# Second layer's channel products, mixing and outputs: one 64-wide tile per image in place of 128-wide blocks that hold two

## The chip, the cores and the metric

The kernel runs on one core of a Trainium2 chip. The metric is the device time of one execution in microseconds; three executions took 310.94, 724.87 and 310.22 us, median 310.94. A separate, profiled execution took 310.58 us; its span from the first to the last instruction is 308.0 us. All data are fp32.

## The reference

Sixteen images of 64 channels and 16 x 16 pixels (N = 256) go through four layers, each `x = x + layer(groupnorm(x))`. The change is in the second layer:

```python
keys    = softmax(Wk x + bk, over N);  queries = softmax(Wq x + bq, over C);  values = Wv x + bv
context = einsum('bkn,bvn->bkv', keys, values)           # 64 x 64 per image
eff     = conv1x1(Wr, br, einsum('bkv,bkn->bvn', context, queries))
# chan_att(L) = softmax( einsum('bcn,bdn->bcd', softmax(L, over N), L), over d ): 64 x 64 per image
att     = chan_att(x) + chan_att(x - G1) + chan_att(G1 - G2)   # G1, G2: blurred x
freq    = einsum('bcd,bcn->bdn', att, queries)
out     = w_dw[0] * eff + w_dw[1] * freq
```

Layer 3 ("het") is a 3 x 3 convolution on some channel groups, layer 4 an attention with 8 heads over quarters of the image.

## The kernel before

Two images share the 128 partitions (channels of image 0 on partitions 0 to 63, of image 1 on 64 to 127); `t` counts the 8 pairs of images, `j = t // 2` counts twos of them, and `g` is the group: `t` 0 to 3 is group 0, 4 to 7 is group 1. In this document and the prediction "an image t" means such a pair of images. Each engine gets its instructions in one fixed order, and a list `SCHEDULE` gives the order of the steps to all of them: group 1 follows group 0 three steps behind. Engines wait for each other by semaphores only. For the second layer the end of the list is: scores1 (t 0, 1), levels1 (j 3), scores1 (t 2, 3), levels_T (j 2), mix1 (j 0), levels_T (j 3), mix1 (j 1), scores1 (t 4, 5), out1 (t 0, 1), scores1 (t 6, 7), out1 (t 2, 3), mix1 (j 2), norm of group 0 for layer 3, mix1 (j 3), out1 (t 4 to 7), norm of group 1, het.

The steps that the change touches:

- `products(t)`, TensorE (L555 to L568): per t the three score matrices and the context, contracted over the 256 pixels in two halves of 128 (k). Each multiplication has 128 weight columns and 128 moving columns, so it also computes the 64 x 64 blocks *between* the two images, which nobody wants. All four results lie in one PSUM bank (4 x 128 columns). A fp32 multiplication shows up as two instructions in the profile.
- `scores_in(t)`, VectorE (L1016 to L1029): adds "apart" (-1e30 between the images, 0 inside an image) to the three score matrices and writes them to SBUF as `att`; multiplies the context by "own" (0 between the images) into `ctxT`; takes the row maxima of `att` and makes the bias of the exponential.
- `channel_softmax(t)`, ScalarE (L1328 to L1333): three exponentials in place in `att`, with row sums.
- `context_out(t)`, TensorE (L570 to L574): `ctxT` times Wr, a 128 x 128 block-diagonal matrix.
- `mixing(j)`, VectorE (L1031 to L1057): for two t in turn, the weighted sum of the three attentions, times w_dw[1], plus the context's product; result `mix2`, 128 x 128 and zero between the images. Ten operations of 128 columns.
- `out_product(t)`, TensorE (L585 to L589): `mix2` times the queries, 256 moving columns.
- `add_out1(t)`, VectorE (L1059 to L1062): adds it to X and takes the statistics (L790) for the next norm.

PSUM banks are handed out in turn by `claim(pe, key, reader's semaphore, value)`: six "bulk" banks and two "small" ones. TensorE, whose queue is in order, waits in `claim` until the bank's last reader has signalled. For products that reader is `ctxT_ready`, VectorE's copy of the context.

After a group's norm (L806 to L824, with a power on GpSimd, L1464, and the result in `xn_pad`), sixteen transfers from SyncE (L1547) and sixteen from ScalarE (L1410) copy shifted rows of `xn_pad` into `region`, group 0 first, half of each engine's sixteen per group; het (L620, L625) of a group waits for its rows. Other lines that appear in the rows: L986 and L987 level maxima, L1307 the level exponentials, L1292 copies of transposed levels, L443 the product y3 of the first layer (128*64 tiles), L709 the products with the values in layer 4 (128*64 tiles), L643 the projections of layer 4, L1393 its exponential.

Of the kernel before, what the change touches and what calls it, by code (L numbers as in the profile page):

```python
# [18 lines left out]
P = 128  # L19
C = 64  # L20
# [3 lines left out]
HW = W * W  # L24
# [3 lines left out]
NK = HW // P  # L28
# [4 lines left out]
NT = NP * AREA  # L33
MASKED = -1e30
ROWS = (W + 2) * W
# [6 lines left out]

CONST = [("pairavg", 128), ("pairavg_by_out", 128), ("to_by_out", 128), ("ident", 128), ("own", 128), ("apart", 128), ("fold", 64), ("lap1", 2 * HW),
         ("lap2", 2 * HW), ("headmask", 4), ("spread", NG * 128), ("spsel", 3 * 128), ("eye4", 32)]
# [76 lines left out]
def program(nc, x_in, const_in, weight_in, param_in, out):  # L121
# [11 lines left out]
    with ExitStack() as ctx:  # L133
# [85 lines left out]
        def tokens_of_pairs():  # L219
# [28 lines left out]
        e_lT = [tokens_of_pairs() for _ in range(3)]  # L248
        att = pairs(384, "p (t s c) -> p t s c", s=3)
        ctxT = pairs(128)  # L250

# [35 lines left out]
                 " qsub_ready qexp_ready   qsm_ready q_mm q_ready "  # L287
                 "lT_mm lT_ready l_mm  a_mm amask_ready ctxT_ready "
                 "amax_ready arec_ready att_ready cw_mm mix_ready y1out_mm  "
# [8 lines left out]
         qsub_ready, qexp_ready, qsm_ready, q_mm, q_ready,  # L298
         lT_mm, lT_ready, l_mm, a_mm, amask_ready, ctxT_ready,
         amax_ready, arec_ready, att_ready, cw_mm, mix_ready, y1out_mm,  # L300
# [44 lines left out]
        def _(pe):  # L345
# [209 lines left out]
            def products(t):  # L555

                j = t // 2
                pe.wait_ge(elT_ready[j // 2], level_step(j % 2, 2) + 1)
                pe.wait_ge(ekT_ready, j + 1)
                pe.wait_ge(vT_ready, j + 1)  # L560
                n = claim(pe, ("a", t), ctxT_ready, t + 1)
                for s in range(3):
                    for k in range(NK):
                        mm(bank(n, s * 128, (s + 1) * 128), e_lT[s][:, k, t, :], lT[s][:, k, t, :],  # L564
                           start=(k == 0), stop=(k == NK - 1))
                for k in range(NK):
                    last = mm(bank(n, 384, 512), vT[:, t, k, :], ekT[:, k, t, :], start=(k == 0), stop=(k == NK - 1))
                last.then_inc(a_mm, 1)  # L568

            def context_out(t):  # L570
                pe.wait_ge(ctxT_ready, t + 1)
                pe.wait_ge(row_ready, 1)
                n = claim(pe, ("cw", t), mix_ready, t + 1, "small")
                mm(bank(n, 0, 128), ctxT[:, t, :], wr_s, start=True, stop=True).then_inc(cw_mm, 1)  # L574

# [9 lines left out]
            def out_product(t):  # L585
                pe.wait_ge(mix_ready, t + 1)
                pe.wait_ge(q_ready, t // 2 + 1)
                n = claim(pe, ("y1out", t), x_ready[1], t + 1)
                mm(bank(n, 0, HW), mix2[:, t, 0:128], q1[:, t, :], start=True, stop=True).then_inc(y1out_mm, 1)  # L589

# [180 lines left out]
        def _(dve):  # L771
# [244 lines left out]
            def scores_in(t):  # L1016

                dve.wait_ge(a_mm, t + 1)
                n = where[("a", t)]
                v.tensor_tensor(att[:, t, :, :], bank(n, 0, 384).rearrange("p (s c) -> p s c", s=3),  # L1020
                                cst("apart").unsqueeze(1).broadcast_to([P, 3, 128]), ALU.add).then_inc(amask_ready, 1)
                v.tensor_tensor(ctxT[:, t, :], bank(n, 384, 512), cst("own"), ALU.mult).then_inc(ctxT_ready, 1)
                dve.wait_ge(amask_ready, t + 1)
                v.tensor_reduce(amax[:, t, :], att[:, t, :, :], X_AXIS, ALU.max).then_inc(amax_ready, 1)

                step(v.reciprocal(lrec[:, t, :], lsum[:, t, :]))
                dve.wait_ge(amax_ready, t + 1)
                v.scalar_tensor_tensor(out=abias[:, t, :], in0=amax[:, t, :], scalar=-1.0, in1=lrec[:, t, :],  # L1028
                                       op0=ALU.mult, op1=ALU.mult).then_inc(arec_ready, 1)  # L1029

            def mixing(j):  # L1031

                c = slice(2 * j, 2 * j + 2)
                ts = (2 * j, 2 * j + 1)
                dve.wait_ge(att_ready, 2 * j + 2)
                recs = mark(v.reciprocal(arec[:, c, :], asum[:, c, :]))
                krecs = mark(v.reciprocal(krec[:, c], ksum[:, c]))
                dve.wait_ge(dve_small, recs)
                at = {}
                for t in ts:  # L1040
                    at[t] = mark(v.tensor_scalar(mix[:, t, 0:128], att[:, t, 0, :], arec[:, t, 0:1], None, ALU.mult))
                for s in (1, 2):
                    for t in ts:
                        dve.wait_ge(dve_small, at[t])
                        at[t] = mark(v.scalar_tensor_tensor(out=mix[:, t, 0:128], in0=att[:, t, s, :],
                                                            scalar=arec[:, t, s:s + 1], in1=mix[:, t, 0:128],
                                                            op0=ALU.mult, op1=ALU.add))
                for t in ts:
                    dve.wait_ge(dve_small, at[t])
                    at[t] = mark(v.tensor_tensor(mix[:, t, 0:128], mix[:, t, 0:128], wt("w1_row"), ALU.mult))  # L1050
                dve.wait_ge(dve_small, krecs)
                for t in ts:
                    dve.wait_ge(cw_mm, t + 1)
                    dve.wait_ge(dve_small, at[t])
                    v.scalar_tensor_tensor(out=mix2[:, t, 0:128], in0=bank(where[("cw", t)], 0, 128),
                                           scalar=krec[:, t:t + 1], in1=mix[:, t, 0:128],
                                           op0=ALU.mult, op1=ALU.add).then_inc(mix_ready, 1)  # L1057
# [161 lines left out]
        def _(act):  # L1219
# [108 lines left out]
            def channel_softmax(t):  # L1328
                act.wait_ge(arec_ready, t + 1)
                for s in range(3):  # L1330
                    last = a.activation(att[:, t, s, :], att[:, t, s, :], ACT.Exp, scale=lrec[:, t, s:s + 1],  # L1331
                                        bias=abias[:, t, s:s + 1], accum_out=asum[:, t, s:s + 1])
                last.then_inc(att_ready, 1)  # L1333
# [260 lines left out]
def constants():  # L1594

    i = np.arange(P)
    same_group = (i[:, None] // 2 == i[None] // 2) * 0.5
    own = (i[:, None] // C == i[None] // C) * 1.0
    y, x = np.divmod(np.arange(HW), W)
# [25 lines left out]
    for b in range(2):  # L1625
        for dx in range(3):
            spsel[3 * b + dx, dx, b * C:(b + 1) * C] = 1.0
    const = pack(CONST, {
        "ident": np.eye(P), "pairavg": same_group, "own": own, "apart": (1.0 - own) * MASKED,
        "fold": np.concatenate([np.eye(64)] * 2), "lap1": chunks(np.eye(HW) - b1), "lap2": chunks(b1 - b2),  # L1630
        "headmask": (i[:, None] % 32 // HD == np.arange(4)[None]) * 1.0,
# [97 lines left out]
```

## Time and profile before

| | |
|---|---|
| median of the runs | 310.94 us |
| profiled execution | 310.58 us |
| its span | 308.0 us |
| TensorE busy (matmul) | 232.2 us, 75% |
| VectorE busy | 194.8 us, 63% |
| ScalarE busy | 131.0 us, 43% |
| GpSimd busy | 35.9 us, 12% |
| chain that ended last | PE 50%; DVE 26%; issue 7%; ACT 5%; DMA 5%; POOL 4% |
| mean granted TensorE clock | 0.887 of full |

By stages, in microseconds from the span's start: the first layer and the start of the second run to about 117, the rest of the second layer to 160.2, layer 3 with its transfers to 187, and layer 4 to 308. PE, DVE, ACT, POOL, SP are the profile's names for TensorE, VectorE, ScalarE, GpSimd and SyncE. Busy times of successive instructions of one engine overlap by up to 0.1 us, so the distance from start to start is the better price of an instruction.

### The profile page before, as it was taken

The numbers are of one execution on the slowest core, as the hardware profiler recorded it, in microseconds if no ns is written. First come the engines' busy times: TensorE is split into PE (matmuls) and PEld (weight loads), VectorE is DVE, ScalarE is ACT, GpSimd is POOL, SyncE is SP. The second block draws the span as 40 slices with busy tenths as digits, with TensorE's granted clock in tenths as the row PEclk, the third lists the DMA queues.
The fourth block names the chain that finished last, engine by engine and source line by source line (L and its number), as shares of the span: only waits on it lengthen the run. The fifth ranks groups of instructions, "written<-read, shape, count | busy, mean of one in ns | idle before, by whom it ended". The sixth has DMA issues, their size and how long they took to land.

```text
span 308.0 us, 5530 instructions
## 1 busy us (share of the span) xinstructions
PE 232.2 (75%) x2032; PEld 141.4 (46%) x2032; DVE 194.8 (63%) x533; ACT 131.0 (43%) x322; POOL 35.9 (12%) x64
## 2 busy tenths in 40 slices
PE   0476997464599869989745378739998998997963
PEld 0355654133274754979622122223564463563541
DVE  3672343537279794797977125576497698686772
ACT  1026579100065577794700022236665565641510
POOL 1750000000100100000011502129001011000000
PEclk9999799755599999997965599997999999997995
DMA  6900000000000000000009990454025025000000
GB/s 223 405 4 3 0 3 0 0 0 2 0 0 0 3 0 0 3 0 2 1 10 228 216 213 5 106 128 108 3 52 124 0 50 135 27 17 20 2 34 34
DMA packets 9642, 16.67 MB, mean 54 GB/s; under 512 B 1936, under 2 KB 8208, under 8 KB 9360
## 3 DMA queue, kind: packets, MB, share of 16 engines
q1 hardware_dynamic: 8848, 13.75, 16.3%
q10 hardware_dynamic: 768, 2.58, 4.0%
q8 instruction: 16, 0.26, 0.4%
q14 instruction: 10, 0.08, 0.1%
HBM read 4.87 MB, written 1.05 MB: 19 GB/s over the span
## 4 chain that ended last, share of the span: by engine, by line
PE 50%; DVE 26%; issue 7%; ACT 5%; DMA 5%; POOL 4%; ACTq 2%; SPq 0%; DVEq 0%; POOLq 0%
PE psum L663 7%; PE psum L518 5%; PE psum L691 4%; DMA region<-xn_pad 4%; PE psum L709 4%; PE psum L681 3%; DVE xn_pad L1136 3%; PE psum L643 3%; DVE smax L1142 3%; POOL small L1464 2%; PE psum L479 2%; PE psum L564 2%; PE psum L414 2%; PE psum L506 2%; PE psum L625 2%
## 5 line engine op out<-in xcount | busy, mean ns | idle before, releaser
L1399 ACT ACTIVATE region<-psum 128x512 f32<-128x512 f32 x32 | 19.0, 594 | 30.8 <-PE psum L691 30.7
L1142 DVE TENSOR_REDUCE smax<-psum 128x8 f32<-128x512 f32 x32 | 21.9, 685 | 12.3 <-PE psum L681 12.3
L1464 POOL TENSOR_TENSOR small<-small 128x4 f32<-128x4 f32 x8 | 8.1, 1018 | 175.4 <-DVE small L808 175.4
L663 PE MATMUL psum<-region,w 128*32 128x512 f32 x160 | 23.0, 647 | 4.1 <-DVE region L1117 4.1
L1393 ACT ACTIVATE region<-region 128x512 f32<-128x512 f32 x32 | 20.1, 627 | 12.8 <-DVE region L1149 12.8
L790 DVE BATCH_NORM_STATS2 small<-X 128x6 f32<-128x256 f32 x32 | 12.5, 422 | 17.5 <-ACT X L1269 16.5
L691 PEld LDWEIGHTS psum<-const,region 128*128 128x128 f32 x128 | 14.3, 145 | 17.8 <-issue 11.8
L1149 DVE TENSOR_TENSOR region<-psum,smax 128x512 f32<-128x512 f32 x32 | 22.1, 690 | 0.6
L691 PE MATMUL psum<-const,region 128*128 128x128 f32 x128 | 21.2, 289 | 1.1 <-ACT region L1399 1.0
L709 PE MATMUL psum<-region 128*64 128x18 f32 x512 | 20.5, 214 | 0.0
L709 PEld LDWEIGHTS psum<-region 128*64 128x64 f32 x512 | 17.4, 137 | 5.2 <-issue 5.2
L1269 ACT ACTIVATE X<-psum,small 128x256 f32<-128x256 f32 x8 | 3.4, 470 | 37.5 <-PE psum L625 37.5
L625 PE MATMUL psum<-region,weight 128*32 128x512 f32 x96 | 12.6, 663 | 6.8 <-DMA region<-xn_pad 6.8
L643 PE MATMUL psum<-region,weight 128*128 128x512 f32 x24 | 13.2, 646 | 3.3 <-DVE small L816 3.3
L354 PE MATMUL psum<-small,const 128*128 128x8 f32 x16 | 3.6, 297 | 15.2 <-DVE small L797 9.9
L1331 ACT ACTIVATE region<-region,small 128x128 f32<-128x128 f32 x24 | 11.6, 488 | 6.8 <-DVE small L1028 6.8
L518 PE MATMUL psum<-region,const 128*128 128x512 f32 x32 | 14.2, 598 | 0.0
L1136 DVE SCALAR_TENSOR_TENSOR xn_pad<-v_pad,small,xn_pad 128x256 f32<-128x256 f32 x32 | 14.1, 487 | 0.0
L564 PE MATMUL psum<-region 128*128 128x128 f32 x96 | 13.3, 293 | 0.0
L564 PEld LDWEIGHTS psum<-region 128*128 128x128 f32 x96 | 12.6, 210 | 0.1
L1279 ACT ACTIVATE region<-psum 8x256 f32<-8x256 f32 x2 | 0.7, 373 | 27.9 <-PE psum L479 27.9
L354 PEld LDWEIGHTS psum<-small,const 128*128 128x128 f32 x16 | 3.3, 251 | 18.5 <-DVE small L797 12.6
(169 smaller groups left out, 490.9 us busy)
## 6 DMA issues: line engine op xcount, KB each, us to landing
region<-v_pad SPq DMA_DIRECT2D x64, 80.0 KB, 2.1
region<-xn_pad SPq DMA_DIRECT2D x16, 157.5 KB, 6.8
region<-xn_pad ACTq DMA_DIRECT2D x16, 157.5 KB, 6.6
weight<-weight_in SPq DMA_DIRECT2D x1, 1376.0 KB, 12.6
const<-const_in SPq DMA_DIRECT2D x1, 1330.0 KB, 9.9
X<-x SPq DMA_DIRECT2D x4, 256.0 KB, 5.2
out<-xn_pad SPq DMA_DIRECT2D x8, 128.0 KB, 1.7
weight<-weight_in SPq DMA_DIRECT2D x1, 918.0 KB, 6.7
```

Of the source, the lines that this page charges most:

```text
L518: last = mm(bank(n), lap[s][:, k, jn * 128:(jn + 1) * 128], xT[:, k, 4 * g:4 * g + 4, :].rearrange("p t c -> p (t c)"), start=(k == 0), st ...
L564: mm(bank(n, s * 128, (s + 1) * 128), e_lT[s][:, k, t, :], lT[s][:, k, t, :], start=(k == 0), stop=(k == NK - 1))
L625: last = mm(bank(n)[32 * q:32 * q + 32, :], hetW[:, q % 2, dx, :], rows[:, q, 2 * jj:2 * jj + 2, 0:W, dx:dx + W], start=False, stop=(dx == 2),
L643: mm(bank(n), wt(w), xn3[:, 2 * j:2 * j + 2, :].rearrange("p t n -> p (t n)"), start=True, stop=True)\
L663: last = mm(bank(n)[32 * c:32 * c + 32, :], w4[:, c % 2, dx, :], v4[:, j % 2, c, :, :, dx:dx + W], start=(dx == 0), stop=(dx == 4), tile_p ...
L691: last = tr(bank(n, q * 128, (q + 1) * 128), e3[:, w % NE, q * 128:(q + 1) * 128], ident)
L709: last = mm(dst[half, a2, b, h:h + 2, :].rearrange("p h e -> p (h e)"), e3T[:, w % NE, at + 64 * c:at + 64 * c + 64], va[:, 4 * t + 2 * a2 ...
L1136: v.scalar_tensor_tensor(out=a, in0=win, scalar=pe_w[:, 5 * PE_ROWS + i:5 * PE_ROWS + i + 1], in1=prev, op0=ALU.mult, op1=ALU.add).then_in ...
L1142: v.tensor_reduce(smax[:, w, :], src, X_AXIS, ALU.max).then_inc(smax_ready, 1)
L1149: v.tensor_tensor(s_sub[:, w % NE, :].rearrange("p (h m) -> p h m", h=HEADS), src, smax[:, w, :].unsqueeze(2).broadcast_to([P, HEADS, AP_] ...
L1393: a.activation(e3[:, u % NE, :], s_sub[:, u % NE, :], ACT.Exp, scale=HD ** -0.5).then_inc(e3_ready, 1)
L1399: a.activation(e3T[:, u % NE, :], bank(where[("e3T", u)]), ACT.Copy).then_inc(e3T_ready, 1)
```

## The change

`products` now issues each multiplication twice, once per image: 64 weight columns and 64 moving columns of that image, K = 128, into the partitions of that image, with the tile position (0, 64 b). The four results take 4 x 64 columns of the bank. `context_out` and `out_product` issue two 64 x 64 multiplications on the diagonal of the array, tile position (64 b, 64 b), both into the same bank. The blocks between images exist no more, so the mask, the multiplication by "own" and the semaphore `amask_ready` go; VectorE takes the maxima straight from PSUM (192 columns) and copies the context (64 columns); ScalarE reads the scores from PSUM. `att`, `ctxT`, `mix`, `mix2` are 64 columns wide per matrix, and so is every operation of `mixing`. The bank of the products is now released by `att_ready` (ScalarE's exponentials). The constants "own", "apart" and "fold" (320 columns, 0.16 MB) are no longer loaded.

```diff
@@ def products(t):
-                n = claim(pe, ("a", t), ctxT_ready, t + 1)
-                for s in range(3):
+                n = claim(pe, ("a", t), att_ready, t + 1)
+                operands = [(e_lT[s][:, :, t, :], lT[s][:, :, t, :]) for s in range(3)] + [(vT[:, t, :, :], ekT[:, :, t, :])]
+                for s, (left, right) in enumerate(operands):
                     for k in range(NK):
-                        mm(bank(n, s * 128, (s + 1) * 128), e_lT[s][:, k, t, :], lT[s][:, k, t, :],
-                           start=(k == 0), stop=(k == NK - 1))
-                for k in range(NK):
-                    last = mm(bank(n, 384, 512), vT[:, t, k, :], ekT[:, k, t, :], start=(k == 0), stop=(k == NK - 1))
+                        for b in range(2):
+                            half = slice(C * b, C * b + C)
+                            last = mm(bank(n, s * C, (s + 1) * C)[half, :], left[:, k, half], right[:, k, half],
+                                      start=(k == 0), stop=(k == NK - 1), tile_position=(0, C * b))
@@ def context_out(t):
-                mm(bank(n, 0, 128), ctxT[:, t, :], wr_s, start=True, stop=True).then_inc(cw_mm, 1)
+                for b in range(2):
+                    half = slice(C * b, C * b + C)
+                    last = mm(bank(n, 0, C)[half, :], ctxT[half, t, :], wr_s[half, half], start=True, stop=True,
+                              tile_position=(C * b, C * b))
+                last.then_inc(cw_mm, 1)
@@ def out_product(t):
-                mm(bank(n, 0, HW), mix2[:, t, 0:128], q1[:, t, :], start=True, stop=True).then_inc(y1out_mm, 1)
+                for b in range(2):
+                    half = slice(C * b, C * b + C)
+                    last = mm(bank(n, 0, HW)[half, :], mix2[half, t, 0:C], q1[half, t, :], start=True, stop=True,
+                              tile_position=(C * b, C * b))
+                last.then_inc(y1out_mm, 1)
@@ def scores_in(t):
-                v.tensor_tensor(att[:, t, :, :], bank(n, 0, 384).rearrange("p (s c) -> p s c", s=3),
-                                cst("apart").unsqueeze(1).broadcast_to([P, 3, 128]), ALU.add).then_inc(amask_ready, 1)
-                v.tensor_tensor(ctxT[:, t, :], bank(n, 384, 512), cst("own"), ALU.mult).then_inc(ctxT_ready, 1)
-                dve.wait_ge(amask_ready, t + 1)
-                v.tensor_reduce(amax[:, t, :], att[:, t, :, :], X_AXIS, ALU.max).then_inc(amax_ready, 1)
+                v.tensor_reduce(amax[:, t, :], bank(n, 0, 3 * C).rearrange("p (s c) -> p s c", s=3), X_AXIS, ALU.max)\
+                    .then_inc(amax_ready, 1)
+                v.tensor_copy(ctxT[:, t, :], bank(n, 3 * C, 4 * C)).then_inc(ctxT_ready, 1)
@@ def mixing(j): every 0:128 becomes 0:C, for example
-                    at[t] = mark(v.tensor_scalar(mix[:, t, 0:128], att[:, t, 0, :], arec[:, t, 0:1], None, ALU.mult))
+                    at[t] = mark(v.tensor_scalar(mix[:, t, 0:C], att[:, t, 0, :], arec[:, t, 0:1], None, ALU.mult))
@@ def channel_softmax(t):
-                    last = a.activation(att[:, t, s, :], att[:, t, s, :], ACT.Exp, scale=lrec[:, t, s:s + 1],
+                    last = a.activation(att[:, t, s, :], bank(where[("a", t)], s * C, (s + 1) * C), ACT.Exp, scale=lrec[:, t, s:s + 1],
```

## Rows read from the trace of the kernel before

**Rows 1.** Chain of waits, 120 to 235 us: start us, duration us, what.

```profile
124.69 0.70 DVE small L986
136.71 0.10 DVE small L1036
155.98 0.36 DVE region L1055
158.80 1.38 DVE xn_pad L824 x4
175.82 11.06 DMA region<-xn_pad
```

**Rows 2.** Timeline of VectorE: start us, us, engine, line, operation, shapes, [idle before <- releaser].

```profile
127.85 0.55 DVE L1020 TENSOR_TENSOR region<-psum,const 128x384 f32<-128x384 f32 x1
128.32 0.28 DVE L1022 TENSOR_TENSOR region<-psum,const 128x128 f32<-128x128 f32 x1
128.51 0.54 DVE L1024 TENSOR_REDUCE small<-region 128x3 f32<-128x384 f32 x1
129.25 0.55 DVE L1020 TENSOR_TENSOR region<-psum,const 128x384 f32<-128x384 f32 x1
137.24 1.13 DVE L1045 SCALAR_TENSOR_TENSOR region<-region,small 128x128 f32<-128x128 f32 x4
139.23 0.18 DVE L1036 RECIPROCAL small<-small 128x6 f32<-128x6 f32 x1
143.82 0.56 DVE L1020 TENSOR_TENSOR region<-psum,const 128x384 f32<-128x384 f32 x1 [1.89 <-PE psum L567]
```

**Rows 3.** Timeline of ScalarE, same columns.

```profile
129.87 0.48 ACT L1331 ACTIVATE region<-region,small 128x128 f32<-128x128 f32 x1
130.34 0.48 ACT L1331 ACTIVATE region<-region,small 128x128 f32<-128x128 f32 x1
138.34 2.04 ACT L1292 ACTIVATE region<-psum 128x512 f32<-128x512 f32 x4
```

**Rows 4.** Groups of instructions, ScalarE, by shape: count, busy us, mean ns, idle.

```profile
L1393 ACT ACTIVATE region<-region 128x512 f32<-128x512 f32 x32 | 20.1, 627 | 12.8 <-DVE region L1149 12.8
L1307 ACT ACTIVATE region<-psum,small 128x256 f32<-128x256 f32 x16 | 7.3, 474 | 3.1 <-DVE small L987 3.1
L1307 ACT ACTIVATE region<-region,small 128x256 f32<-128x256 f32 x8 | 4.0, 501 | 3.9 <-DVE small L987 3.9
```

**Rows 5.** Timeline of TensorE: second layer, then one y3 and one values3 group.

```profile
127.15 1.50 PE L564 MATMUL psum<-region 128*128 128x128 f32 x12
128.49 0.61 PE L567 MATMUL psum<-region 128*128 128x128 f32 x4
139.21 0.77 PE L574 MATMUL psum<-wr_s,region 128*128 128x128 f32 x4 [2.02 <-DVE region L1055]
...
41.42 1.08 PE L443 MATMUL psum<-region,weight 128*64 128x256 f32 x8
42.44 1.58 PE L403 MATMUL psum<-region,const 32*128 32x256 f32 x24
...
212.96 0.65 PE L709 MATMUL psum<-region 128*64 128x18 f32 x16
213.54 1.13 PE L643 MATMUL psum<-region,weight 128*128 128x512 f32 x2
```

**Rows 6.** Busy time by window: length, engines' busy us (x instructions), clock, DMA share, GB/s.

```profile
127.85:139.20 11.35, 9.34 (x84) 9.05 (x83) 11.07 (x40) 10.01 (x38) 0.00 (x0) 1.00 0.00 1
139.20:142.60 3.40, 3.39 (x18) 3.40 (x19) 2.73 (x13) 1.78 (x4) 0.00 (x0) 0.58 0.02 5
162.00:174.00 12.00, 4.58 (x8) 2.10 (x8) 6.36 (x24) 0.00 (x0) 4.48 (x2) 0.50 1.02 223
212.00:230.00 18.00, 17.56 (x239) 9.89 (x219) 12.94 (x24) 11.55 (x20) 3.62 (x7) 1.00 0.16 39
```

**Rows 7.** Timeline of SyncE's transfers, 158 to 190 us.

```profile
160.21 15.96 SPq L1547 DMA_DIRECT2D region<-xn_pad  x16
```

More of the change, by code:

```diff
@@ L33 @@
 NT = NP * AREA
-MASKED = -1e30
 ROWS = (W + 2) * W
@@ L40 @@
 GN_EPS = 1e-5
-CONST = [("pairavg", 128), ("pairavg_by_out", 128), ("to_by_out", 128), ("ident", 128), ("own", 128), ("apart", 128), ("fold", 64), ("lap1", 2 * HW),
+CONST = [("pairavg", 128), ("pairavg_by_out", 128), ("to_by_out", 128), ("ident", 128), ("lap1", 2 * HW),
          ("lap2", 2 * HW), ("headmask", 4), ("spread", NG * 128), ("spsel", 3 * 128), ("eye4", 32)]
@@ L248, in program @@
         e_lT = [tokens_of_pairs() for _ in range(3)]
-        att = pairs(384, "p (t s c) -> p t s c", s=3)
-        ctxT = pairs(128)
+        att = pairs(3 * C, "p (t s c) -> p t s c", s=3)
+        ctxT = pairs(C)
         mix, mix2 = e_l[0], e_l[1]
@@ L287, in program @@
                  " qsub_ready qexp_ready   qsm_ready q_mm q_ready "
-                 "lT_mm lT_ready l_mm  a_mm amask_ready ctxT_ready "
+                 "lT_mm lT_ready l_mm  a_mm ctxT_ready "
                  "amax_ready arec_ready att_ready cw_mm mix_ready y1out_mm  "
@@ L298, in program @@
          qsub_ready, qexp_ready, qsm_ready, q_mm, q_ready,
-         lT_mm, lT_ready, l_mm, a_mm, amask_ready, ctxT_ready,
+         lT_mm, lT_ready, l_mm, a_mm, ctxT_ready,
          amax_ready, arec_ready, att_ready, cw_mm, mix_ready, y1out_mm,
@@ L1044, in mixing @@
                         dve.wait_ge(dve_small, at[t])
-                        at[t] = mark(v.scalar_tensor_tensor(out=mix[:, t, 0:128], in0=att[:, t, s, :],
-                                                            scalar=arec[:, t, s:s + 1], in1=mix[:, t, 0:128],
+                        at[t] = mark(v.scalar_tensor_tensor(out=mix[:, t, 0:C], in0=att[:, t, s, :],
+                                                            scalar=arec[:, t, s:s + 1], in1=mix[:, t, 0:C],
                                                             op0=ALU.mult, op1=ALU.add))
@@ L1049, in mixing @@
                     dve.wait_ge(dve_small, at[t])
-                    at[t] = mark(v.tensor_tensor(mix[:, t, 0:128], mix[:, t, 0:128], wt("w1_row"), ALU.mult))
+                    at[t] = mark(v.tensor_tensor(mix[:, t, 0:C], mix[:, t, 0:C], wt("w1_row")[:, 0:C], ALU.mult))
                 dve.wait_ge(dve_small, krecs)
@@ L1054, in mixing @@
                     dve.wait_ge(dve_small, at[t])
-                    v.scalar_tensor_tensor(out=mix2[:, t, 0:128], in0=bank(where[("cw", t)], 0, 128),
-                                           scalar=krec[:, t:t + 1], in1=mix[:, t, 0:128],
+                    v.scalar_tensor_tensor(out=mix2[:, t, 0:C], in0=bank(where[("cw", t)], 0, C),
+                                           scalar=krec[:, t:t + 1], in1=mix[:, t, 0:C],
                                            op0=ALU.mult, op1=ALU.add).then_inc(mix_ready, 1)
@@ L1597, in constants @@
     same_group = (i[:, None] // 2 == i[None] // 2) * 0.5
-    own = (i[:, None] // C == i[None] // C) * 1.0
     y, x = np.divmod(np.arange(HW), W)
@@ L1628, in constants @@
     const = pack(CONST, {
-        "ident": np.eye(P), "pairavg": same_group, "own": own, "apart": (1.0 - own) * MASKED,
-        "fold": np.concatenate([np.eye(64)] * 2), "lap1": chunks(np.eye(HW) - b1), "lap2": chunks(b1 - b2),
+        "ident": np.eye(P), "pairavg": same_group,  "lap1": chunks(np.eye(HW) - b1), "lap2": chunks(b1 - b2),
         "headmask": (i[:, None] % 32 // HD == np.arange(4)[None]) * 1.0,
```

## The prediction

> **What bounds the kernel now.** I first followed the chain of waits through the second layer [rows 1]. From 124.69 us, when the last mirrored level arrives, VectorE holds the chain: level maxima, scores, mixing. TensorE holds it from 139.21 [rows 5] to the end of products(7) at 150.5, VectorE again up to the last normalised image of group 0 (158.80 + 1.38 = 160.18). There the queue of transfers takes over: the shifted rows of group 0 are issued at 160.21 [rows 7], the sixteen DMA engines are then full (share 1.02 from 162 to 174, [rows 6]), and the last rows of group 1 land at 186.88 [rows 1]. Group 1 asked for its rows only at 170.5, yet the chain passes through the landing: 26.7 us of saturated transfer hang on the *start* of group 0. So a change in this stage is worth what it moves 160.18, as long as group 1 comes before group 0's transfers run dry at about 174, a slack of 3.5 us. Behind 186.88 nothing is edited and I move it as a block.
>
> The VectorE timeline [rows 2] has the prices and the one place where VectorE waits (1.89 us before 143.82, for TensorE). The TensorE timeline [rows 5] has a 2.02 us wait for `mixing` at 139.21, and behind it a granted clock of 0.58 of full, mostly the 1.2 GHz level, until 142.60 [rows 6].
>
> **The change, part by part.**
>
> *scores_in, VectorE, 8 times.* Now: 0.47 (mask), 0.20 (own block), 0.46 (maximum), then reciprocal and bias; 127.85 to 129.25 is 1.40 us [rows 2]. From 0.20 for 128 columns to 0.47 for 384, a column costs 1.05 ns. After: the mask is gone, the maximum reads 192 columns (0.46 - 192 x 1.05 ns = 0.26; that it now reads PSUM is bounded by the mask add, which read 384 PSUM columns in the time of the 384-column maximum from SBUF), the copy 64 (0.13), the two small ones 0.28 as now. Together 0.67 with the waits between them, 0.73 less.
>
> *mixing, VectorE, 4 times.* Its first operation starts at 136.62 by the timeline (136.71 in the chain) and the next mixing's at 139.23, 2.6 us [rows 1, 2]. Ten operations lose 64 columns, 0.067 each: 1.94. Two images alternate, so a dependent operation starts two later, after 0.39; it needs its predecessor's 0.28 (0.35 now, from 1.13 less three steps of 0.26) and a few hundredths. No new stall. With three mixings ahead of 160.18, VectorE loses 8 x 0.73 + 3 x 0.67 = 7.8 us of work there.
>
> *channel_softmax, ScalarE, 24 exponentials.* Now 0.48 each with its accumulator read [rows 3]. 512 to 256 SBUF columns saves 0.126 us, 0.49 ns a column, and the same exponential is 0.03 cheaper from PSUM [rows 4]; 64 fewer columns and that give 0.42 (bounds 0.35 and 0.48), 1.25 an image for 1.44.
>
> *products, TensorE, 8 times.* Each multiplication is two instructions. Now 16 of 128 columns: twelve from 127.15 to 128.49 [rows 5], 112 ns each, 1.79 us an image. After, 32 instructions with 64 weight columns and 64 moving ones. One alone should take half, 56 ns: 1.79 again. The gain exists only if the two column halves run at once. Rows for it: y3 (128*64 tiles, 256 moving columns, halves in turn) does eight in 42.44 - 41.42 = 1.02, 128 ns each, where 256 columns at the rate of products would take 224; values3 (64 weight columns, 18 moving) does 16 in 213.54 - 212.96 = 0.58, 36 ns each, the turn to the next kind of tile included [rows 5]. Full overlap would be 56/2 = 28 ns. I take 33, a little under values3, since the turn is shared by 32 here: 1.06 us an image. Ends: 28 ns (0.9) and 56 ns (1.79).
>
> *context_out* stays at about 0.2 us (four instructions of 64 columns for two of 128). *out_product* is now two instructions of 256 columns, 0.45 an image at the rate of products; its two diagonal halves have 256 columns each, so 0.45 if they overlap and 0.9 if not. No row shows two row blocks writing one bank at once; y3 is nearest (two column halves, one bank), so 0.45. The Trainium skill (TensorEngine Tiling (Array Packing), Restrictions and Gotchas) says that different row tiles cannot access the same PSUM bank at the same time. By that rule it would be 0.9, and no run here shows it; the rival below has its time.
>
> *Banks.* The scores' bank is now held until ScalarE has taken the exponentials, not until VectorE's copy. Queued behind that wait are queries(1) and products(2), six bulk claims later. Priced below.
>
> *Constants.* 320 columns fewer, 0.16 MB of a load that nobody waits for: 0.
>
> **The new order, laid out at full clock.** VectorE: scores 0 at 127.93 to 128.60, scores 1 to 129.27, levels of pair 3 (3.15 us, unchanged) to 132.42. ScalarE: exponentials of 0 and 1, 128.65 to 131.15. TensorE could start products(2) near 129.8 but gets its bank at 131.2: the new wait, 1.4 us there, and the new hold eats all of TensorE's early gain. Products 2 and 3 end at 132.25 and 133.3; scores 2 and 3 end at 133.1 and 134.1. ScalarE has 3.2 us of copies and level exponentials, then exponentials 2 and 3 from 134.4 to 136.9, and two copies to 137.9, which products(4) needs (now 138.34 + 0.96 = 139.3 [rows 3]). mixing(0) ends at 136.05, mixing(1) at 138.9. TensorE: context and queries in the gap, products 4 and 5 137.95 to 140.1, outputs 0, 1 to 141.0, queries(3) 141.45, products 6, 7 to 143.55, outputs 2, 3 to 144.45. VectorE: scores 4, 5 to 140.95, outputs 0, 1 (1.75 us) to 142.7, scores 6, 7 to 144.4, outputs 2, 3 with aggregation to 146.6, mixing(2) to 148.5, then 3.84 us as now (156.34 to 160.18): 152.35. Gain 7.8.
>
> The clock: TensorE has gaps of 0.8 and 1.0 us from 135.3 to 138 in place of one of 2.0, so a dip to 1.2 GHz behind them can come again. It would double products 4 and 5, 2.1 us, of which VectorE hides a little: gain 6. Between them I take 7.0. The profiled execution took 310.58 (span 308.0), 0.36 below the median: 303.6, and 303.9 as a median. Group 1's normalisation comes 8 us earlier too, inside its slack.
>
> **Rivals.**
> *A. The halves do not overlap in time* (chance 0.13). Products stay at 1.79. Then a3 ends at 134.7, mixing(1) at 139.45, products 4 to 7 and the outputs fill 137.95 to 147.3, VectorE's 160.18 becomes 155.1: gain 5.0, about 306. Only out_product serial, as in the skill's rule: TensorE is late by 0.9 per pair of images, half of it behind VectorE's work, gain near 6: 305. For A: no row has both sizes at 64. Against: y3 and values3.
> *B. The 1.2 GHz level holds from the first gap on* (0.14). Products 2.1, outputs 0.9, queries 0.9: products 7 end at 149.0, group 0 is normalised at 157.9: gain 2.3, 308.6. For: TensorE has less work in these microseconds than before, and the clock stays at 0.50 from 162 to 174, where it has little work [rows 6]. Against: the attention of layer 4, mostly narrow tiles, runs at 1.00 from 212 to 230 [rows 6].
> *C. Slower* (0.05). A and B together: twice as many instructions, one after another and at 1.2 GHz, where TensorE sets the pace, from 137.95. Products 3.58, outputs 1.8: group 0 at 166.9, 317.7. It decides from 2.85 us an image, 89 ns an instruction: then the four products eat what the rest gained.
> *D. The transfers do not follow* (0.05). If group 1's request at 170.5 set the landing and not the bandwidth, the gain would be that of group 1, 8 us: 303. Against: the DMA share stays at 1 in between.
> *E. The edit is hidden* (0.03): ScalarE, busy 10.01 of the 11.35 us from 127.85 to 139.20 [rows 6], sets the pace. Its own saving is 8 x 0.19 = 1.5: 309.4.
>
> **How the numbers follow.** My forecast has 0.60 (gain 6.0 to 8.5, 302.4 to 304.9). A measurement of this kernel tells about 2%, 6.2 us, from no change: 304.7. Faster: 0.85 of 0.60, D, and a little of A, 0.58. Slower: C and unknowns, 0.05. Same: 0.37. The range runs from 301.8 (products at 0.9 us, full clock) to 308.7 (B); outside are C, E and luck.
>
> **What would show it.** Products of one image 1.0 to 1.2 us apart, not 1.8; scores_in 0.67 from start to start; mixing 1.95; L986 of pair 3 no longer right behind the scores of image 1 by TensorE's doing; queries(1) or products(2) waiting for ScalarE's exponentials; the first issue of shifted rows near 153 and the last landing 26.7 later. I am wrong if the clock row between 137 and 150 reads 0.5, if the outputs take 0.9 an image, or if the stretch from the first issue to the last landing changes by more than 1 us.

## The result and the profile after

The changed kernel takes 302.5 us (median of 4 runs, 301.29 to 303.75) against 310.79 before (4 runs, one of them 724.87 us): a ratio of 0.973, 95% interval 0.969 to 0.976, or 8.3 us less. The forecast was 303.9. The profiled execution took 303.56 us, its span 301.8 us. Medians here and below are over all runs of a kernel, while ratios leave out those more than 1.5% above its fastest, of which experiments 3, 4, 7 and 8 (the kernel without the exchange) have some; the profiled executions of 3 and 4 are among them.

To compare traces that start the second layer at slightly different times, I cut each at three events: VectorE's first level maximum of image pair 2 (124.69 before), the first transfer of shifted rows (160.21), and TensorE's first het instruction for group 1 that reads these rows (186.92). The stretch between the first two is called the stage. The first line is from before, the others from after:

```profile
186.92 2.78 PE L625 MATMUL psum<-region,weight 128*32 128x512 f32 x24 [1.52 <-DMA region<-xn_pad]
...
125.49 0.69 DVE L994 TENSOR_REDUCE small<-psum 128x2 f32<-128x512 f32 x1 [5.85 <-PE psum L531]
...
152.97 15.25 SPq L1553 DMA_DIRECT2D region<-xn_pad  x16
...
179.62 2.78 PE L633 MATMUL psum<-region,weight 128*32 128x512 f32 x24
```

| | first maximum | to first transfer | to het of group 1 | from there to the end |
|---|---|---|---|---|
| before | 124.69 | 35.52 | 26.71 | 121.1 |
| after | 125.49 | 27.48 | 26.65 | 122.2 |

The edited stage lost 8.04 us and the transfers kept their length. Unedited code gave 0.8 us back ahead of the stage and 1.1 us behind it, so that the span is 6.2 us shorter.

One part of the gain lies outside the span. The time less the span is 1.75 to 1.85 us in the ten runs of the changed kernel (the four here and the six of experiment 7), and 1.75 to 3.06 us, 2.4 on average, in 65 runs of the kernel before: some 0.6 us of the 8.3. In the profiled executions it is 1.76 for 2.58. No run shows why. It is not the constants alone, since experiment 5 loads all of them and has 1.8 to 1.9 as well.

The first view of the trace after is the chain of waits, from 120 to 200 us (start us, duration us, what):

```profile
129.45 1.51 ACT region L1337 x7
...
135.16 2.32 ACT region L1337 x12
137.48 0.98 ACT region L1298 x2
...
138.50 2.09 PE psum L566 x64
140.59 1.01 PE psum L595 x8
...
148.61 0.28 DVE region L1061
...
151.56 1.38 DVE xn_pad L832 x4
...
167.90 11.67 DMA region<-xn_pad
```

Where VectorE had held the chain up to 139.21 [rows 1], ScalarE holds it now, from the first exponential at 129.45 to the copies that products(4) needs at 138.46 (L1337 is the exponential, L1298 the copies). The end is the same queue of transfers.

TensorE's timeline in the same stretch (start us, us, engine, line, shapes, count, [idle before <- releaser]); L566 is products, L595 out_product, L586 queries, L576 context_out:

```profile
130.86 0.63 PE L586 MATMUL psum<-const,region 128*128 128x128 f32 x4 [0.62 <-ACT region L1337]
132.02 2.08 PE L566 MATMUL psum<-region 128*64 128x64 f32 x64 [0.53 <-ACT region L1337]
...
136.95 0.52 PE L576 MATMUL psum<-wr_s,region 64*64 64x64 f32 x8 [0.42 <-DVE region L1061]
...
140.52 1.08 PE L595 MATMUL psum<-region 64*64 64x256 f32 x8
141.53 0.66 PE L586 MATMUL psum<-const,region 128*128 128x128 f32 x4
142.12 2.08 PE L566 MATMUL psum<-region 128*64 128x64 f32 x64
```

The products of two images t take 2.04 us by the chain (142.19 to 144.23), 32 ns an instruction and 1.02 us an image, for 1.79 before. The first two lines show the new wait for a bank, 0.62 and 0.53 us, both on ScalarE's exponentials. The 2.02 us wait for mixing [rows 5] is down to 0.42.

VectorE, the lines that answer to [rows 2], and two exponentials of ScalarE for [rows 3]:

```profile
128.65 0.35 DVE L1028 TENSOR_REDUCE small<-psum 128x3 f32<-128x192 f32 x1
128.92 0.21 DVE L1030 COPY region<-psum 128x64 f32<-128x64 f32 x1
...
129.33 0.35 DVE L1028 TENSOR_REDUCE small<-psum 128x3 f32<-128x192 f32 x1
...
146.93 0.16 DVE L1042 RECIPROCAL small<-small 128x6 f32<-128x6 f32 x1
...
148.59 0.48 DVE L1061 SCALAR_TENSOR_TENSOR region<-psum,small,region 128x64 f32<-128x64 f32 x2
```

```profile
129.84 0.39 ACT L1337 ACTIVATE region<-psum,small 128x64 f32<-128x64 f32 x1
...
130.23 0.40 ACT L1337 ACTIVATE region<-psum,small 128x64 f32<-128x64 f32 x1
```

scores_in is 129.33 - 128.65 = 0.68 us from start to start (1.40 before), mixing 146.93 to 148.89, 1.96 (2.6 before), an exponential 0.39 (0.48 before).

The granted clock by window (us, length, busy us of the engines, clock, DMA share, GB/s):

```profile
140.00:142.00 2.00, 2.00 (x33) 1.34 (x28) 1.73 (x10) 1.49 (x8) 0.00 (x0) 1.00 0.04 8
...
155.00:162.00 7.00, 4.35 (x12) 1.55 (x12) 4.90 (x20) 0.00 (x0) 1.01 (x1) 0.50 1.05 234
...
194.00:206.00 12.00, 8.57 (x60) 4.34 (x60) 6.71 (x17) 4.31 (x8) 7.35 (x8) 0.57 0.53 123
```

The low level of 139 to 142.6 us [rows 6] is not there: the products of images 4 to 7 ran at full clock. From 155 to 162 us, while the transfers run, the clock is at its low level, as it was before [rows 6]. The last line belongs to the 1.1 us lost behind the stage: layer 4 starts at 0.57 of full clock, where the same stretch of the kernel before (201.3 to 213.3 us) had 0.86. In the chain of waits two places hold the whole loss: two projections take 2.05 us for 1.36, and the 32 instructions of L689 (L681 before) 1.45 us for 1.06. The projections on TensorE's timeline, before and after:

```profile
207.30 1.36 PE L643 MATMUL psum<-region,weight 128*128 128x512 f32 x2 [3.25 <-DVE small L816]
```

```profile
200.00 2.05 PE L651 MATMUL psum<-region,weight 128*128 128x512 f32 x2 [2.60 <-DVE small L824]
```

### The profile page after: what moved, and what is told of

It is laid out like the page before. It is cut to its first block, busy times and chain, and to the rows that moved or that the text cites. A ratio compares the mean times of both kernels' runs of the same rounds, so it can differ in the third digit from the quotient of the medians.

```text
span 301.8 us, 5842 instructions
## 1 busy us (share of the span) xinstructions
PE 228.6 (76%) x2192; PEld 133.9 (44%) x2192; DVE 187.1 (62%) x525; ACT 128.6 (43%) x322; POOL 35.9 (12%) x64
## 3 DMA queue, kind: packets, MB, share of 16 engines
q10 hardware_dynamic: 768, 2.58, 4.1%
## 4 chain that ended last, share of the span: by engine, by line
PE 51%; DVE 23%; ACT 7%; issue 7%; DMA 5%; POOL 4%; ACTq 2%; SPq 0%; DVEq 0%; POOLq 0%
PE psum L671 7%; PE psum L517 5%; PE psum L699 4%; DMA region<-xn_pad 4%; PE psum L717 4%; PE psum L689 3%; PE psum L651 3%; DVE xn_pad L1142 3%; DVE smax L1148 3%; POOL small L1470 2%; PE psum L478 2%; PE psum L413 2%; PE psum L505 2%; PE psum L633 2%; PE psum L388 2%
## 5 line engine op out<-in xcount | busy, mean ns | idle before, releaser
L1405 ACT ACTIVATE region<-psum 128x512 f32<-128x512 f32 x32 | 19.0, 593 | 32.7 <-PE psum L699 32.6
L699 PE MATMUL psum<-const,region 128*128 128x128 f32 x128 | 21.9, 297 | 1.1 <-ACT region L1405 1.0
L651 PE MATMUL psum<-region,weight 128*128 128x512 f32 x24 | 13.9, 676 | 2.6 <-DVE small L824 2.6
L689 PE MATMUL psum<-region 32*64 32x256 f32 x256 | 10.3, 433 | 1.3 <-ACT X L1275 1.3
L1298 ACT ACTIVATE region<-psum 128x512 f32<-128x512 f32 x20 | 11.0, 624 | 0.7 <-PE psum L495 0.7
L1518 POOL COPY region<-v_pad 128x256 f32<-128x256 f32 x16 | 6.3, 436 | 40.9 <-PE psum L660 37.1
## 6 DMA issues: line engine op xcount, KB each, us to landing
region<-xn_pad SPq DMA_DIRECT2D x16, 157.5 KB, 7.3
region<-xn_pad ACTq DMA_DIRECT2D x16, 157.5 KB, 7.2
```

What stands on the lines that cost most here:

```text
L651: mm(bank(n), wt(w), xn3[:, 2 * j:2 * j + 2, :].rearrange("p t n -> p (t n)"), start=True, stop=True)\
L689: last = mm(bank(banks[r], a2 * 256, a2 * 256 + 256)[64 * c:64 * c + 64, :], q3[rows, j % 2, a, :], km[rows, j % 2, a, :, :].rearrange("p ...
L699: last = tr(bank(n, q * 128, (q + 1) * 128), e3[:, w % NE, q * 128:(q + 1) * 128], ident)
L1405: a.activation(e3T[:, u % NE, :], bank(where[("e3T", u)]), ACT.Copy).then_inc(e3T_ready, 1)
```

## The experiments

There were eleven runs: ten more kernels, and the changed kernel again. All times are medians, all ratios to the kernel before on the same chip. The positions come from one profiled execution each and are given in the table at the end of this section.

**1. Do the two halves overlap?** The loop over the image moved outwards:

```diff
-                for s, (left, right) in enumerate(operands):
-                    for k in range(NK):
-                        for b in range(2):
+                for b in range(2):
+                    for s, (left, right) in enumerate(operands):
+                        for k in range(NK):
```

> The changed kernel, but in products all 16 instructions of one image half come before the 16 of the other, so that neighbours are on the same column half of the array; everything else as in the changed kernel. Theory (the two halves run at once only when they alternate): an image goes from 1.02 us (its 64 instructions for two images took 2.04) to 1.8 us, the sixteen transfers of group 0 start near 155.5 us in place of 152.97, and the time is about 305 us. Rival (32 ns is the rate at which such small instructions can be issued, whichever half they go to): 1.02 us an image, no change, 302.5 us.

Measured 306.4 us, ratio 0.986 (0.982 to 0.991). TensorE's timeline:

```profile
137.68 3.41 PE L566 MATMUL psum<-region 128*64 128x64 f32 x64
```

The same 64 instructions start over 3.33 us (the next kind starts at 141.01), 52 ns each in place of 32. So 32 ns does not come with the size of the instructions. It is two column halves at work together, and it needs neighbouring instructions to be on different halves. 1.67 us an image is a little under the 1.8 expected. The stage was 3.2 us longer than in the changed kernel: four products on the chain make 4 x 0.65 = 2.6 of it, and the rest I did not trace.

**2. TensorE's part alone.** The changed products in the kernel before, with the mask and the 128-wide layout kept:

```diff
+                            last = mm(bank(n, s * 128 + C * b, s * 128 + C * b + C)[half, :], left[:, k, half], right[:, k, half],
+                                      start=(k == 0), stop=(k == NK - 1), tile_position=(0, C * b))
```

> The kernel before with the changed products alone: 64-wide tiles per image, written to their places in the 128-wide layout; the mask and all VectorE and ScalarE work stay 128 wide. Theory (VectorE sets the pace up to mixing(1), TensorE only between 139 and 150): products 1.02 us an image, the first transfers start 2 to 3 us earlier than 160.21, about 308.3 us. Rival (TensorE's work is what the stage is worth): 8 x 0.77 = 6.2 us less, 304.6 us.

Measured 310.53 us, ratio 1.000 (0.997 to 1.003). The stage is 2.49 us shorter, as the theory had it, but the time is the same, and not the 308.3 us that the theory gave. Here are its TensorE timeline and its clock in one window:

```profile
133.99 1.90 PE L567 MATMUL psum<-region 128*64 128x64 f32 x32 [1.67 <-ACT region L1293]
...
140.22 0.72 PE L575 MATMUL psum<-wr_s,region 128*128 128x128 f32 x4 [1.17 <-DVE region L1056]
...
185.33 4.45 PE L626 MATMUL psum<-region,weight 128*32 128x512 f32 x24
```

```profile
133.00:139.00 6.00, 5.01 (x52) 4.73 (x52) 5.83 (x22) 6.00 (x24) 0.00 (x0) 0.72 0.01 3
```

A faster TensorE waits more (1.67 and 1.17 us, for 2.02 before), and behind the first wait its clock falls (0.72 from 133 to 139 us, 1.00 before). Behind the transfers, het of group 1 takes 4.45 us in place of 2.78, and from its start to the end it is 123.7 us for 121.1: this execution loses there the 2.5 us that the stage gained. Over whole executions the mean granted clock of its 10 runs is 0.860, that of 65 runs of the kernel before 0.880. Among those 65 runs the time falls by about 0.9 us for 0.01 of mean clock (a fitted line, correlation -0.59). If clock and time go together in the same way here, 0.02 of clock is worth an estimated 1.8 us, most of the 2.5; a correlation does not show it.

**3. VectorE's and ScalarE's part alone.** The changed kernel with the old products:

```diff
+                for s in range(3):
+                    for k in range(NK):
+                        mm(bank(n, s * 128, (s + 1) * 128), e_lT[s][:, k, t, :], lT[s][:, k, t, :],
+                           start=(k == 0), stop=(k == NK - 1))
...
+                v.tensor_reduce(amax[:, t, :], bank(n, 0, 384).rearrange("p (s c) -> p s c", s=3)[:, :, 0:C], X_AXIS, ALU.max)\
```

> The changed kernel with TensorE's products as before (128 x 128, 1.79 us an image); VectorE and ScalarE take 64 columns of each result, so for the second image of a pair they take the block between images: its values are not the reference's, only the time is read. Theory: it keeps most of the gain, first transfers near 155.2 us, about 305.8 us (5 us less than before). Rival (TensorE's work is what the stage is worth): about 309 us.

Measured 308.31 us, ratio 0.991 (0.988 to 0.994). The stage is 3.81 us shorter, where rival A's layout had 5.0, and the time 2.4 us. The theory had 305.8 us, the rival 309: the rival is nearer on the time, the theory on the stage. In the profiled execution, one of the three longest of the ten (310.23 us), the gain is lost behind the stage:

```profile
184.55 4.48 PE L632 MATMUL psum<-region,weight 128*32 128x512 f32 x24
```

Het of group 1 took 4.48 us in place of 2.78, at the low clock. Whether the shorter runs had this too is not shown.

2.49 and 3.81 make 6.3. Both together made 8.04. Either engine alone hides part of the other's gain.

**4. The bank's hold alone.** One word in the kernel before:

```diff
-                n = claim(pe, ("a", t), ctxT_ready, t + 1)
+                n = claim(pe, ("a", t), att_ready, t + 1)
```

> The kernel before with one edit: the bank of products is released by the exponentials and not by VectorE's copy. Theory: queries(1) and products(2) wait for ScalarE, products(2) starts at 132.3 in place of 131.12, VectorE then waits about 0.7 us once, 311.5 us. Rival 1: hidden, 310.8. Rival 2: the same wait comes back at every later image, 313 us or more.

Measured 311.78 us, ratio 0.995 (0.991 to 0.999): median and ratio lean opposite ways, so the time decides nothing. In the trace TensorE waits 0.22 and 0.80 us for the exponentials, and products(2) starts 7.81 us behind the first maximum instead of 6.43. In that execution the low clock of 139 us stayed away, so its stage (35.22 us) is to be held against experiment 5 (34.07), not against the kernel before. The hold then costs about 1.1 us by these two executions, not hidden, and not repeated at later images.

**5. The low clock behind the wait.** The last transposes before TensorE's 2.02 us wait are done five times over:

```diff
-                for q in range(2):
+                for _, q in [(r, q) for r in range(5 if (j, s) == (3, 2) else 1) for q in range(2)]:
                     for k in range(NK):
```

> The kernel before with one edit: the last transposes before TensorE's 2.02 us wait at 139.21 are done five times over, so that TensorE is busy while it would have waited. Theory (the 1.2 GHz level behind that wait is a consequence of the wait): the clock from 139 to 143 reads 1.00, the first transfers start 1.0 to 1.7 us earlier, about 309.5 us. Rival (the level falls wherever it likes, or its cost is hidden): no change, 310.8 us.

```profile
139.20:142.60 3.40, 3.14 (x29) 3.04 (x28) 3.14 (x15) 2.17 (x5) 0.00 (x0) 1.00 0.00 0
```

The clock reads 1.00 where [rows 6] had 0.58, and the first mixing ended at the same distance from the first maximum (14.5 us). The stage is 1.45 us shorter. In time, 309.83 us, ratio 0.997 (0.993 to 1.0004): in the direction expected, not beyond noise. So of the 8.04 us, some 1.5 are this dip; that the change removed it by shortening the wait to 0.42 us follows from this, and was not tried by itself.

**6. The mask alone.**

```diff
-                v.tensor_tensor(att[:, t, :, :], bank(n, 0, 384).rearrange("p (s c) -> p s c", s=3),
-                                cst("apart").unsqueeze(1).broadcast_to([P, 3, 128]), ALU.add).then_inc(amask_ready, 1)
...
+                v.tensor_reduce(amax[:, t, :], bank(n, 0, 384).rearrange("p (s c) -> p s c", s=3), X_AXIS, ALU.max)\
```

> The kernel before, all tiles 128 wide, but without the mask add: the maximum and the exponentials read the score matrices from PSUM, with the bank held as in the changed kernel. The blocks between images enter the softmax, so the values are not the reference's; only the time is read. Theory (VectorE's 0.47 us an image counts up to mixing(1) and at the last scores, TensorE's products in between hide the rest): first transfers 2 to 2.5 us earlier than 160.21, about 308.5 us. Rival (the mask is most of the gain): 8 x 0.47 = 3.8 us less, 307.0 us or below.

Measured 310.89 us, ratio 1.000 (0.997 to 1.004); the stage is 1.93 us shorter. VectorE now waits for products at all images but the first, 0.2 to 0.3 and 0.75 us in turn, for three such waits before (1.89, 0.29 and 0.25). Two lines of its timeline:

```profile
143.66 0.56 DVE L1020 TENSOR_REDUCE small<-psum 128x3 f32<-128x384 f32 x1 [0.26 <-PE psum L567]
...
145.45 0.56 DVE L1020 TENSOR_REDUCE small<-psum 128x3 f32<-128x384 f32 x1 [0.75 <-PE psum L567]
```

3.8 us less VectorE work bought 1.9 us of stage and nothing in the time, where the theory had 308.5 us and the rival 307.0: het of group 1 took 4.25 us at the low clock.

**7. What hangs on the start of group 0's transfers?** In the changed kernel, group 0's norm goes ahead of the mixing of images 4 and 5 in the order list:

```diff
+at = SCHEDULE.index(("mix", 0, 1))
...
+SCHEDULE[at:at + 2] = [("norm", 2, 0), ("mix", 0, 1)]
```

> The changed kernel with two neighbours in the order list exchanged: the norm of group 0 for layer 3 comes before the mixing of images 4 and 5 on all engines. The work is the same. Theory (the time hangs on the start of group 0's transfers): they start about 2 us earlier than 152.97 us, the last rows of group 1 land 26.6 us after that, and the time falls by about 2 us, to 300.4 us. Rival (group 1's normalised images, which come no earlier, set the landing): 302.5 us, unchanged.

Measured 303.48 us (6 runs, 299.23 to 304.18), ratio 0.968 (0.960 to 0.975), beside 303.33 (0.975, 0.971 to 0.979) for the changed kernel on the same chip:

> The changed kernel once more, as the measure for norm_before_mix on this chip and for what one execution differs from the next. Expected: 302.5 us; 152.97 us for the first transfer, give or take the start of the stage; the rest of the spread from the granted clock in code that nobody edited.

The medians are equal. The ratio of the exchange is 0.007 lower, some 2 us, but rests on three of its six runs, so its time is undecided. The changed kernel repeated itself: stage 27.47 us, 301.5 us span. The exchange moved the first transfer by 2.1 us as expected (25.35 us of stage), and group 1's rows were no longer waited for. TensorE's timeline, het of group 0 and of group 1:

```profile
165.51 5.28 PE L638 MATMUL psum<-region,weight 128*32 128x512 f32 x24 [6.19 <-DMA region<-xn_pad]
...
177.71 4.30 PE L638 MATMUL psum<-region,weight 128*32 128x512 f32 x24
```

Now the later chain is the other one: the landing of group 0, het at 1.2 GHz (5.28 us, 2.78 at full clock), norm, het of group 1. From the first transfer to het of group 1 it took 27.58 us, not 26.6. Neither the theory nor the rival had this.

The landing itself has two lengths. Het of group 0, which waits for its rows, starts 15.2 to 15.4 us behind the first transfer in the changed kernel and in experiments 1, 3, 5, 7 and 8, but after 13.9 to 14.1 us in the kernel before and in 2, 4, 6 and 9. The kernels with the short one are just those whose profiled execution has 2.6 to 3.1 us outside its span, the others have 1.8 to 1.9. No run shows what divides them. With a landing 1.3 us earlier the second chain of experiment 7 would take about 26.3 us, less than the first.

**8. The same, with TensorE kept busy while it waits for rows.**

```diff
-                mm(bank(n), cst("to_by_out"), X[:, 2 * j:2 * j + 2, :].rearrange("p t n -> p (t n)"), start=True, stop=False)
+                for i in range(7 if j == 0 else 1, 0, -1):
+                    mm(bank(n), cst("to_by_out"), X[:, 2 * j:2 * j + 2, :].rearrange("p t n -> p (t n)"), start=True, stop=i > 1)
```

> norm_before_mix with the same filling of TensorE's wait for the rows. Its group 1 did not wait for rows any more: het of group 0 took 5.28 us and of group 1 4.30 us at the low clock, between 165.5 and 182.0. Theory: both go to 2.8 us, the rows of group 1 set the pace again, het of group 1 starts near 176.8 in place of 177.7 and ends 2.4 us earlier, about 300.5 us. Rival (the low clock comes back elsewhere and takes it away): 303 us.

> The changed kernel with one edit: the first multiplication of het for group 0 is done seven times over, which keeps TensorE busy while it waits for the shifted rows of group 0 (159.2 to 168.2 us in the changed kernel). Theory (the landing of group 1's rows, 26.6 us behind the first transfer, is the later of two chains, the other being group 0's landing plus het at 1.2 GHz and the norm behind it): het of group 0 goes from 4.35 to 2.8 us, the het of group 1 starts at the same 179.5 us, and only what the clock gives later counts: 302 to 303 us. Rival (TensorE at 1.2 GHz is on the chain): 1.5 us less, 301.5 us or below.

With the exchange: 300.71 us (299.13 to 301.7), ratio 0.967 (0.964 to 0.970). Without it: 304.99, 0.980 (0.976 to 0.983). First the kernel with the exchange, then the one without:

```profile
164.72 2.78 PE L639 MATMUL psum<-region,weight 128*32 128x512 f32 x24 [0.94 <-DMA region<-xn_pad]
...
175.91 4.48 PE L639 MATMUL psum<-region,weight 128*32 128x512 f32 x24 [1.53 <-DMA region<-xn_pad]
```

```profile
168.19 2.78 PE L634 MATMUL psum<-region,weight 128*32 128x512 f32 x24
...
179.40 5.35 PE L634 MATMUL psum<-region,weight 128*32 128x512 f32 x24 [1.55 <-DMA region<-xn_pad]
```

In both, group 0's het runs at full clock and group 1's waits for its rows again, 26.48 and 26.44 us behind the first transfer. That is the saturated queue, now with its start 2.1 us earlier, and the two-chain reading holds. But in both the low clock moved to group 1's het. Without the exchange the filling costs 1.7 us against the run of experiment 7 and 2.5 against the first result: it saved nothing on the chain and the clock's fall came where it hurt. With it, mean clock 0.901 and the best time of all kernels here, 10.3 us under the kernel before, where the theory had 300.5 us. Why the clock stayed high there and not in the other is open.

**9. The exchange in the kernel before.** The same two lines as in 7.

> The kernel before with the same exchange in the order list: norm of group 0 before the mixing of images 4 and 5. There mixing is 2.6 us and not 1.95. Theory: first transfers near 157.6 us in place of 160.21, of which the low clock in het takes about one microsecond back: 309.3 us. Rival: group 1 sets the landing, unchanged at 310.8 us.

Measured 311.71 us (12 runs), ratio 1.002 (0.9993 to 1.005). The stage is 2.38 us shorter and het of group 1 starts 2.0 us earlier against the first maximum (60.20 for 62.23 us). It then takes 5.35 us in place of 2.78 and the gain is gone. The theory (309.3 us) had half of that; the rival has the time (310.8), but not the way to it, since het of group 1 did start earlier. Here the wait before it, the request of group 1 and the transfers' share in between:

```profile
183.81 5.35 PE L630 MATMUL psum<-region,weight 128*32 128x512 f32 x24 [0.83 <-DMA region<-xn_pad]
...
169.51 0.52 ACTq L1415
...
168.00:170.00 2.00, 0.04 (x1) 0.00 (x0) 1.44 (x5) 0.00 (x0) 0.46 (x1) 0.50 0.74 146
170.00:172.00 2.00, 1.26 (x8) 0.40 (x12) 0.00 (x0) 0.00 (x0) 2.00 (x1) 0.50 0.68 179
```

Het of group 1 waits for its own rows, so the second chain is not what makes 27.06 us out of 26.7. Group 1 asked 12.76 us behind the first transfer (10.3 before), and by then the queue was running dry: the share falls to 0.74 and 0.68. In experiment 8 with the exchange it asked about 11.6 us behind, the share stayed at 1.0 or more, and the stretch was 26.48 us.

| kernel | first maximum | to first transfer | to het of group 1 | from there to the end |
|---|---|---|---|---|
| 1 halves in blocks | 123.88 | 30.69 | 26.48 | 122.1 |
| 2 TensorE alone | 125.70 | 33.03 | 26.60 | 123.7 |
| 3 VectorE, ScalarE alone | 125.22 | 31.71 | 27.62 | 123.8 |
| 4 hold alone | 125.06 | 35.22 | 26.71 | 121.9 |
| 5 filled wait | 125.08 | 34.07 | 26.60 | 122.3 |
| 6 mask alone | 126.18 | 33.59 | 26.51 | 123.4 |
| 7 norm before mix | 124.78 | 25.35 | 27.58 | 123.5 |
| 8 with the wait filled | 124.06 | 25.37 | 26.48 | 123.8 |
| 8 without the exchange | 125.46 | 27.50 | 26.44 | 123.5 |
| 9 exchange in before | 123.61 | 33.14 | 27.06 | 123.7 |

The last column was 121.1 in the kernel before. No edit reaches that code, and all eleven kernels with another stage lose 0.8 to 2.7 us there; what differs is het of group 1 and the start of layer 4 at the low clock.

## Why the prediction was right, point by point

*What bounds.* Right for the stage and the transfers: from the first transfer to het of group 1 it is 26.4 to 26.7 us in nine of the twelve kernels, whose first transfers lie between 149.43 and 160.28 us, and experiment 8 moved the start alone. It has two limits that I had wrong. The second chain through group 0's het lay closer than I had seen (27.6 us at the low clock) and is the longer one in experiments 3 and 7. And the slack of group 1's request, which I gave as 3.5 us, was used up by the 2.5 us of experiment 9, where the queue ran dry and the stretch took 27.06 us. Besides, the code behind 186.88, which I moved as a block, became 1.1 us slower.

*Prices.* scores_in 0.68 for 0.67; mixing 1.96 for 1.94; products 32 ns for 33, 1.02 us for 1.06; an exponential 0.39 for 0.42. out_product: eight instructions of 256 columns in 1.01 us, 126 ns each, 0.50 us an image for 0.45. One by one they would take 224 ns each, 0.9 us. So two row blocks that write one bank did run together here, on the reading that a 64*64 tile alone would go at that rate; no run has the diagonal halves one after the other. The Trainium skill (TensorEngine Tiling (Array Packing), Restrictions and Gotchas) says that different row tiles cannot access one PSUM bank at the same time. The 126 ns speak against it for this case, in which the two write different partitions of the bank.

*The layout.* Group 0 normalised 27.45 us behind the first maximum, laid out 152.35 - 124.69 = 27.66. The bank's hold cost TensorE 0.62 + 0.53 = 1.15 us where I had 1.4.

*The clock.* I took half of a dip, 0.8 us, off the layout's 7.8. No dip came, and the layout at full clock was the better forecast: 8.04. The size that I missed was at the other end. Of these 8.04 the profiled execution kept 6.2 in its span, since unedited code was slower by 1.9, and it gained 0.8 outside. In time that is 310.58 - 303.56 = 7.0 us, just what I forecast for it, and this is luck: my 7.0 is a stage 1.0 too small, with neither of the other two terms. The medians of the runs say 8.3.

*The signs.* The clock from 137 to 150 us reads 0.91, not 0.5; the outputs take 0.50 us an image, not 0.9; the stretch to het of group 1 changed by 0.06 us. The wait for the exponentials came at both places named. One sign did not show: the level maxima of pair 3 still start right behind the scores of image 1.

*The rivals.* A is refuted by the 1.02 us an image, and experiment 1 pays its price: forced apart, the halves cost 1.67 us an image, the stage loses 3.2 us of its 8.04, and the time comes to 306.4, where A said 306. B did not happen in the stage, but its mechanism is real in het and at the start of layer 4, and it is what ate experiments 2, 6 and 9. C needs both. D is refuted by experiment 9, where group 1's request came no earlier (45.90 us behind the first maximum for 45.81) and its het started 2.0 us earlier; its grain is the request that comes too late in experiment 9. E is refuted in its number and right in its engine: ScalarE does hold the chain from 129.45 to 138.46 now. The change made it faster by 0.27 us an image, and my layout had run through it.

*The parts.* The prediction gave no price for either half alone. The experiments add that the halves are worth far less alone: TensorE's part nothing in time, VectorE's and ScalarE's 2.4 us, both 8.3. The diagonal tiles of context_out and out_product and the shorter load of constants were not run by themselves.

## What to carry to other kernels

Where two engines take turns in holding the chain, lay out the new order event by event. Sums per engine (7.8 us on VectorE, 6.2 on TensorE) don't say what the two halves will be worth alone; that the first came near the 8.04 of both together is chance, since the chain ran through ScalarE and TensorE as well. Small matmuls on different column halves of the array overlapped here only where neighbours in the queue alternated between them (32 ns an instruction, else 52). And once a stage is faster, see in the trace what TensorE's clock does behind it: in experiments 2, 6 and 9 the gain of the stage went in a het that nobody edited and that now ran at the low clock. So compare stages as well as whole times.

## What the runs showed of the hardware

- 128*64 tiles with 64 moving fp32 columns: 32 ns an instruction when the halves alternate, 52 ns when they don't. 64*64 tiles on the diagonal with 256 moving columns, both into one bank: 126 ns an instruction, for 224 at the rate of the 128 x 128 form.
- An exponential with its accumulator read, from start to start: 0.39 us for 64 columns from PSUM, 0.48 for 128 columns from SBUF.
- Two kernels whose stages differ by 2.5 us took the same time (310.53 and 310.74 us), with mean granted clocks of 0.860 and 0.880.
- Keeping TensorE busy through a wait kept the clock at 1.00 behind it in all three kernels where it was tried. In the two that fill the wait for the rows, the low level then appeared at het of group 1.
- 32 transfers of 157.5 KB on two queues kept the 16 DMA engines full, and the last landed 26.4 to 26.7 us behind the first in nine kernels. When the second group's were asked for 12.76 us behind the first, the share fell to 0.7 in between.
